# A decoder layer on one core: four order tables that interleave its stages are rewritten

## What is computed

```
x = layernorm(x + self_attention(x))        # 16 heads of 8; softmax(y y^T / sqrt 8) x, then @ weight (16*128 x 128)
x = layernorm(x + cross_attention(x, ctx))  # 16 heads of 8, window |i-j| <= 64, biases, output projection
x = layernorm(x + local(x))                 # two layers l = 0, 1, each:
#   h = shift_token(x); q, k, v = split(h @ wqkv[l]); 8 heads of 64; l2norm(q)*qs, l2norm(k)*ks; rotary
#   x = x + softmax(causal window 64)(q k^T) v @ wo[l]
#   h = layernorm(shift_token(x))*g + b; a, g = split(h @ w1[l] + b1[l]); x = x + (a * gelu(g)) @ w2[l] + b2[l]
```

## Time and profile before

| quantity | value |
|---|---|
| median of 3 runs | 1411.89 us |
| the profiled execution: its own time, its span | 1411.89 us, 1410.1 us |
| TensorE busy | 1314.7 us, 93% |
| VectorE busy | 1053.0 us, 75% |
| ScalarE busy | 982.9 us, 70% |
| GpSimd busy | 756.9 us, 54% |
| mean granted TensorE clock | 0.971 |

### The profile page before, as it was taken

How to read it: one execution, slowest core, us unless ns; L and a number is a source line. 1 busy time by engine, 2 the same in 40 slices (tenths; PEclk the granted TensorE clock), 3 DMA queues, 4 the chain that set the end, 5 groups by cost and what they waited for, 6 DMA issues and landing times. The chain is left out here.

```text
span 1410.1 us, 39538 instructions
## 1 busy us (share of the span) xinstructions
PE 1314.7 (93%) x12472; PEld 915.3 (65%) x12472; DVE 1053.0 (75%) x3190; ACT 982.9 (70%) x2694; POOL 756.9 (54%) x843
## 2 busy tenths in 40 slices
PE   6789999999999999999999999999999999998964
PEld 3456666667666667666666776666666766666653
DVE  2567887777888878778787877878787788878542
ACT  2357777777777777777777777777777777776553
POOL 1036565655656565555565655655565565655442
PEclk9899999999999999999999999999999999999785
DMA  5000000000000000000000000000000000000000
GB/s 164 11 6 4 5 8 6 6 6 4 5 2 6 6 6 6 4 6 2 6 6 6 6 4 6 4 4 6 6 6 6 4 4 4 6 5 3 3 3 4
DMA packets 22220, 12.55 MB, mean 9 GB/s; under 512 B 5879, under 2 KB 21025, under 8 KB 22177
## 3 DMA queue, kind: packets, MB, share of 16 engines
q1 hardware_dynamic: 21600, 10.96, 2.7%
q10 hardware_dynamic: 576, 1.05, 0.2%
HBM read 9.91 MB, written 2.10 MB: 9 GB/s over the span
## 5 line engine op out<-in xcount | busy, mean ns | idle before, releaser
L1192 POOL TENSOR_TENSOR local_rn<-local_sc,half_neg 128x8 f32<-128x8 f32 x128 | 211.2, 1650 | 162.4 <-DVE local_sc L1040 162.4
L855 ACT ACTIVATE local_e<-local_ps,local_bias,local_rn 128x128 f32<-128x128 f32 x512 | 233.0, 490 | 22.1 <-DVE local_bias L1053 22.1
L1213 POOL TENSOR_TENSOR local_e<-local_e,local_rd 128x512 f32<-128x512 f32 x128 | 133.3, 1041 | 130.5 <-DVE local_rd L1057 130.5
L589 PE MATMUL self_ps<-self_z,self_e 128*128 128x129 f32 x1024 | 149.9, 288 | 3.1 <-ACT self_e L782 2.1
L609 PE MATMUL local_ps<-wz,self_kT 128*128 128x512 f32 x256 | 143.1, 641 | 1.8 <-ACT self_kT L788 1.0
L974 DVE SCALAR_TENSOR_TENSOR self_y<-self_ps,self_rd,self_y 128x128 f32<-128x128 f32 x448 | 132.7, 343 | 8.1
L589 PEld LDWEIGHTS self_ps<-self_z,self_e 128*128 128x128 f32 x1024 | 130.3, 194 | 11.9 <-issue 3.0
L855 ACT ACTIVATION_READ_ACCUMULATOR local_e<-local_ps,local_bias,local_rn 128x1 f32 x512 | 121.5, 237 | 0.0
L935 DVE TENSOR_REDUCE cross_neg<-cross_ps 128x4 bf16<-128x512 f32 x128 | 82.5, 686 | 38.9 <-PE cross_ps L502 38.9
L1048 DVE TENSOR_REDUCE local_m<-local_ps 128x4 f32<-128x512 f32 x128 | 87.1, 680 | 32.6 <-PE local_ps L512 32.6
L835 ACT ACTIVATE local_sq<-local_ps 128x512 f32<-128x512 f32 x128 | 76.4, 597 | 46.1 <-PE local_ps L668 45.2
(11 more groups left out here) (172 smaller groups left out, 3383.5 us busy)
## 6 DMA issues: line engine op xcount, KB each, us to landing
self_xin<-x SPq DMA_DIRECT2D x32, 64.0 KB, 1.8
cross_cin<-ctx_in SPq DMA_DIRECT2D x32, 64.0 KB, 1.7
out<-local_out SPq DMA_DIRECT2D x32, 64.0 KB, 1.6
wqkv_s<-wqkv SPq DMA_DIRECT2D x2, 768.0 KB
wz<-w_heads ACTq DMA_DIRECT2D x4, 256.0 KB, 5.8
w_r<-w SPq DMA_DIRECT2D x2, 341.0 KB
con<-consts SPq DMA_DIRECT2D x1, 640.0 KB, 6.4
wo_s<-wo SPq DMA_DIRECT2D x2, 256.0 KB
```

The source lines that it names most:

```text
L589: last = nc.tensor.matmul(bank[:, 129 * j:129 * j + 129], s.e[:, h0 + j, :], s.z[:, h0 + j, :], start=True, stop=True)
L855: nc.scalar.activation(s.e[:, a, p, :], bank[:, 128 * p:128 * p + 128], ACT.Exp, bias=s.bias[:, a, p:p + 1], scale=s.rq[:, a, p:p + 1], ac ...
L1192: nc.gpsimd.tensor_tensor(s.rn[:, heads], s.sc[:, heads], half_neg[:, 0:LH], ALU.pow).then_inc(done, STEP)
L1213: nc.gpsimd.tensor_tensor(s.e[:, a, :, :], s.e[:, a, :, :], s.rd[:, a, :].unsqueeze(2).to_broadcast([128, LH // 2, 128]), ALU.mult)\
```

## The change

Only the four tables change; each string holds the same letters as before, in another order.

```diff
 ORDER_TENSOR = (
-    "ONOAAONABSPPBABPZCSZBSACAZSDSCZSCBBSCSECSDDSSDCSDEEMCCECME")
+    "ONOAAONABSPPBABPZSZBCSAAZCSDSCZSCBBSCSECSDDSSDCSDEEMCCECME")
```

More of the change, by code:

```diff
@@ L70 @@
 ORDER_TENSOR = (
-    "ONOAAONABSPPBABPZCSZBSACAZSDSCZSCBBSCSECSDDSSDCSDEEMCCECME")
+    "ONOAAONABSPPBABPZSZBCSAAZCSDSCZSCBBSCSECSDDSSDCSDEEMCCECME")
 ORDER_VECTOR = (
-    "NNNONOAAAAAPBBPBSSBBSASCCCDCCDDDCCOBSPSDSEEDESESSESSSESSSDSMMSMCCSMPCCEC")
+    "NNNONOAAAAAPBBBPSSABSBOSCCCDDCCDDCCBDSSSEDESESESSSSESESSDMPSMMCPCSMCCESC")
 ORDER_SCALAR = (
-    "KOAANBSAPBASBCZZBACAYSZSSZDSSBBDDCDEECDDCEEDCCEEEM")
+    "KOAANBSAPBASZZBBCAAZSYCSSDZDSSBBDCDECEDDCEEDCCEEEM")
 ORDER_GPSIMD = (
-    "NSBNASAAABABBABBDDECESMMPCO")
+    "NNSBASAAAABABBBBDDCEEMPMSCO")
 def shape_constants():
```

## The result

| | before | after |
|---|---|---|
| median of the paired runs | 1411.89 us (7 runs, 1407.84 to 1415.17) | 1423.21 us (7 runs, 1418.68 to 1424.40) |
| ratio, 95% interval | | 1.0074 (1.0055 to 1.0092) |
| profiled execution: time, span | 1411.89, 1410.1 us | 1424.68, 1422.9 us |
| one iteration of the hardware loop, mean of 20 | 40.854 us | 41.126 us |
| VectorE busy, ScalarE busy | 1053.0, 982.9 us | 1074.4, 978.9 us |

The change makes the kernel slower by 11.3 us, 0.74%, against a forecast of 1417.5 us. The interval, 5.5 to 9.2 thousandths, is 8 to 13 us. The mean iteration is taken from one start of S4 on TensorE (L559) to the start 20 iterations later. It grew by 0.27 us: 26 times, 7.0 us. The profiled executions are 12.8 us apart; what the loop does not explain of that lies in the written-out iterations, mostly in the fill.

The account below looks back on a forecast made before the run. TensorE, busy 39.76 of 40.86 us per iteration, was taken as the bound. +0.23 (covering -0.07 and late K), -0.13, +0.03 and +0.08 give +0.21 us, 27 times 5.7 us: 1417.5 us, range 1406.5 to 1425.5.

Parts of the forecast that it names:

- signs that I had named for being wrong: L559 without its wait, L589's start showing no wait for self_e, or an unnamed wait on L627, L675 or VectorE's B4.
- Up to L559: VectorE's run to the last self maximum: one seam closes, -0.07 us per iteration, between 0 and -0.15.
- K behind the load: ScalarE's C2 copies, now behind the exp table load, give K 0.2 us late; costed at nothing, hidden by S7.
- drain beside the load: Rival: a drain as long as the table load follows it, S7 some 0.9 us later; 1442 us, chance 0.02.
- D2 ahead of S6: ScalarE's self exps start later, so TensorE's S7 (L589) is late: +0.23 us per iteration, between +0.15 and +0.28.
- C6's wait given back: Cross L532 no longer waits for ScalarE's C3 behind both D2 and D3: -0.13 us, between 0 and -0.13.
- C6 to D7: Stretch where ScalarE delivers the transposed weights about 0.03 later than TensorE wants: +0.03 us, between 0 and +0.1.
- E1: Step in C6 to D7: its exps on ScalarE follow a later VectorE step, ScalarE idling some 0.7 us more.
- M4 later by 0.26, of which 0.08 shows: P4 and S18 ahead of M4 on VectorE delay L734 by 0.26 us; only +0.08 shows at L718, 0 to +0.15.
- the faster one: Rival: L559's and C6's waits go, S7's is hidden; net -0.2 us per iteration, 1406.5 us, chance 0.17.
- K for C3: Rival: C2's copies end later than summed, TensorE waits for K; further 0.3 us per iteration, 1425.5 us, chance 0.13.
- No change: Rival: S7's lag is the short 0.05 us, load hidden, C6 gives back 0.13; 1412 to 1414.6 us, chance 0.20.

Follow-up runs that it names:

- b5_behind_s4: Kernel before, VectorE's table alone changed: A6 ahead of S3, B5's product behind the last self maximum; 1407.96 us, 0.9967 of before.
- tuned: b5_behind_s4 plus ScalarE's S3 and Z3 ahead of the table load, C3 ahead of D3, TensorE's L665 ahead of one MLP step; 1390.00 us, 0.9832 of before.
- m2_back: Changed kernel with the whole end of VectorE's string put back (S19 ahead of M4, P4 behind it); 1430.13 us, 1.0135 of before.

## Why the prediction was right, and where it fell short

The direction and the main mechanism, D2 making S7 late, were right: with D2 taken out 0.22 of the 0.27 us goes. The length of an iteration was forecast at 41.07 against 41.13 measured. The time was 5.7 us short: 1.3 of it lies in the loop's terms, about 3 (with 2 of doubt) in a part that I had costed at nothing, and the rest, about 1.3, is within the scatter between runs.

Two of the signs that I had named for being wrong came true by the list of waits: L559 lost most of its wait, and L589 shows none in the loop. The signs were badly chosen; the mechanism was not wrong. L559 still starts 0.15 us behind the last maximum, and L589 starts 0.78 behind its exp, with K made early even with a listed wait. A sign that rests on a listed wait of a tenth or two tests the list's lower edge.

- *Up to L559*, -0.07: measured -0.04. VectorE still sets L559. It isn't kept, as said, since S7 sets the time.
- *K behind the load*: K was forecast 0.2 late. Z4 was late by 0.10, and nothing of it reached the iteration (K made early: 41.126 still). There was no drain beside the load either: S3 ends at 696.53 and the load starts at 696.54; it ends at 697.82, the tiny activation starts at 697.84 and C2 at 697.95. The Trainium skill, "ScalarE: Activation LUTs", What ACT_TABLE_LOAD costs, states a load of about 1283 ns and a drain of about 1380 ns for every switch to a different set; the load's 1.28 us agrees, the drain does not show.
- *D2 ahead of S6*, +0.23: the steps came out as counted, S6 at 3.18 behind S4 (3.19 forecast) and S7 0.78 behind that. The size was off. S7 starts 0.78 behind the start of its exp, the upper bound of my sum (694.65 - 693.87), where I took a value inside; and measured from Z1 it comes 0.32 later than before, above the bound of 0.28, since S4 on ScalarE is 0.05 later than I summed (690.73 in before's times). Another 0.07 comes between the first and the second group of L589, after a start that had to wait, which I had no term for. Together the shift grows by 0.39 from Z1 to S8. Taking D2 out gives only 0.22 back: in the mean of 20 iterations S7 is then still 0.07 late, which is K's lateness without its cover, C6 gives back 0.08, and 0.08 is lost from C6 to P1, where it was 0.03.
- *C6's wait given back*, -0.13: measured -0.13. L512 to L532 is 0.34 now.
- *C6 to D7*, +0.03: measured 0.00, though ScalarE idles 1.03 us for E1's bias.
- *M4 later by 0.26, of which 0.08 shows*: L734 late by 0.29; at P1 (L742) 0.03 of it is left. The 0.26 was luck. I counted P4 at 0.28 less a part of the gap between C8 and C9, and P3 at 0.05; P4 alone costs nothing, as it starts before the reciprocal has ended and C9 comes no later, P3 costs 0.15 and S18 behind C9 0.12.
- *The sum*: -0.04 + 0.02 + 0.10 + 0.24 + 0.07 - 0.13 + 0.03 = +0.29 in this iteration, and 0.27 in the mean of 20, where I had +0.21. The upper bounds of my terms add up to +0.53, not to the +0.45 that I wrote.
- *Fill and drain at nothing, within 2 us*: this fell short, by the 3 us of the medians. The profiled execution lost 4.9 us in its fill and about 1 in its drain. After's profile has a stretch at 1.2 GHz near 105 us. One between 96 and 113 us stands in every profile with the new tables in the fill except the one where VectorE's whole end was put back, and not in before's, in those with the new loop alone or in that of D2 put into before. But it stands also in those of the last two kernels (b5_behind_s4 and tuned), which have almost the old tables and lose no time outside the loop (351.1 and 348.1), and the one without it (m2_back) loses as much as after (353.5). So the clock explains this profile's fill, but that it is the cause of the edges' 3 us is not shown, and what tips it stays open.

The rivals: the faster one failed at its own condition, for VectorE had to reach its last maximum 0.2 us earlier and reached it 0.04 earlier (6.37 us behind Z1, where it was 6.41). K for C3 failed because 0.10 of lateness lay inside the cover. No change needed the short lag at S7, and S7 had the long one.

## What to carry to other kernels

When one engine is busy 97% of each iteration, compare the starts of its instructions before and after, instruction by instruction. The list of waits shows 11.6 us at a place that costs 1, and nothing in the loop at L589, where 8 are lost (0.31 in each of 26 iterations). A step put ahead of another in a queue costs its length less the gap it fills, so order steps such that a short ready one stands where the next would wait for its input. And written-out fill iterations deserve a term of their own, judged by the medians of many executions: there TensorE is not busy all the time, and stretches at half clock came and went from profile to profile, with the same tables too.

## What the hardware showed beyond that

- Two groups of small matmuls on separate row groups (L537, then L521 in the program) start interleaved in the record, 16 in 0.34 us, if the second group's input is there when the first begins. With K 0.1 us late they run nearly one behind the other: L532 to Z4 takes 1.63 us in place of 1.53.
- A reciprocal of 128x128 takes 0.96 us on VectorE where a multiplication takes 0.29, and the multiplication that reads it starts 0.08 to 0.09 us behind its end (709.28 against 709.20). A step that does not read it starts ahead of its end: P4 at 717.79, where the reciprocal ends at 717.87, and the multiplication at 717.96 is no later for it.
- The clock is at 1.2 GHz in stretches of the fill (in before between 32 and 39 us and between 62 and 69) and again in the drain: the last 29 us of both profiles have a granted clock of 0.50. In between, from 125 to 1300 us, it is 1.00 in both.
